# A top-p threshold search with two sums instead of three in the first of two attention steps

## The chip, the cores and the metric

The program runs on one core of one Trainium2 chip. The metric is the device time of one execution in microseconds (us), the median of several. The core has five engines that run side by side and meet at semaphores: TensorE (PE in the profile), VectorE (DVE), ScalarE (ACT), GpSimd (POOL) and SyncE (SP, which here only starts transfers).

## The reference

Four graph layers over 2048 nodes with 128 features follow each other. The change lies in the second, which runs two attention steps:

```python
q = X @ W1.T @ W2.T; k = X @ W3.T
probs = softmax(q @ k.T)                      # 2048 x 2048
idx = argsort(-probs); sp = take_along_axis(probs, idx)
cs = cumsum(sp)
keep_sorted = cs - sp < 0.9                   # top-p: the largest entries until 0.9 is reached
A = probs * mask;  A = A / A.sum(-1)
for n in range(2):   A = top_p(Xa);  Xf = R @ Xf;  Xa = A @ Xa;  Z += Xf @ U1[n].T + Xa @ U2[n].T
```

So in each step every one of the 2048 rows needs the value at which the sum of its larger entries first reaches 0.9 of the row.

## The kernel before

A step is cut into four **groups** of 512 rows, and a group into four **tiles** of 128 rows by 2048 columns (index `k`); `gi` counts the groups, 0 to 3 in the first step and 4 to 7 in the second. The exponentials of a group lie in the buffer EA or EB by turns, so one group's search can run while the previous group is still being multiplied.

For each tile PE makes the logits (line 713, instructions at line 710), DVE takes the row maxima (`row_max`, 1636), and ACT takes the exponential and its row sum (`exponential`, 1187). A first guess of the threshold comes from the mean logit and the row sum (`guess_gap`, 1661; ACT's `guess`, 1204; `guess_first`, 1672).

Then comes the **search**. A sum is the mass of a tile's entries at or above the trial threshold; on DVE it is one pass over 128x2048 (`mass_above`, 1808), on ACT it is two passes, Relu and Sign (`sums_below`, 1216). After the first sum a model of the slope gives a step (`first_step`); after the second and the third a secant gives it (`next_step`, 1877). The flag m == 1, which only the third has, makes the secant lean: the surplus is multiplied by 1.2 or 0.8, whichever is larger, and 7 times the threshold is added (`AHEAD`), so that the threshold comes to lie a few entries above the root. `REACH` and `REACH_HI` limit a step; the limits are constants of one instruction.

In the first group of a step (`BOTH`, gi 0 and 4) `first_sums` (1925) and `third_sum` (1900) run one after the other: three tiles on DVE, the fourth on ACT. In the other groups the first two sums are taken ahead, while the group before is finished: three tiles on ACT and the last on DVE; the third sum then takes all four tiles on DVE.

After the search (`group`, 2049) `under` writes, tile by tile, the entries below the threshold to `cands[k]`; before it writes there, DVE waits until PE has turned the previous group's `cands[k]` (`e_turned`). Eight-wide maxima over eight sets of 256 columns, and four rounds of them, give the 32 largest of these entries; a running sum finds the crossing among them (`crossing_checked`, 1969). `doubtful` (2035) raises a flag where the crossing is not safely inside: threshold at or below the root, no crossing among the first 31, or a set of 256 that may hold more than eight of the wanted entries. One flagged row of the group sends DVE through `surely` (2015), a bracketed search with as many rounds as it needs, each of four sums, followed by four passes of `under`, four of maxima, four of `masked` and four of ties. `masked` (1982) writes the kept entries and their sum, and `kept_ok` releases PE.

The **order of the work** is written out by hand on each engine. While DVE searches group gi, PE multiplies group gi - 1 (`attend`, 756): per tile 16 transposes (line 527; `turns(0)` to `turns(3)`) and 16 products (788), with ACT copying each set of four transposes (1060). Between them PE makes the logits of group gi + 1, one tile per tile (each needs the exponential of the tile before it), and DVE's row maxima of that group are spread over the search: the one of tile 1 (`next_max(1)`) sits inside `third_sum`, that of tile 2 ahead of the first `under`, that of tile 3 after the second `under`. In group 0 there is no earlier group to multiply. There PE runs **units** (line 728; `unit_sums`, 580, instructions at 593) of another product, whose operand SP reloads in two halves per unit, and it makes the logits of group 1 between two units. ACT's order in group 0 is: exponential of a tile of group 1, then the copies of a unit.

Of the kernel before, what the change touches and what calls it, by code (L numbers as in the profile page):

```python
# [7 lines left out]
ALU = mybir.AluOpType  # L8
# [11 lines left out]
G = BK // P  # L20
NB = NT // G
# [7 lines left out]
REACH = 1.2  # L29
REACH_HI = 1.95  # L30
SOFT = (40.0, 20.0)
AHEAD = 7.0
ROUNDING = 2e-5
# [61 lines left out]
def gnn_kernel(nc, x, adj, W0, b0, W1, W2, W3, U1, U2, ln_g, ln_b, L2W, L3W, b3, out):  # L95
# [18 lines left out]
    with ExitStack() as ctx:  # L114
# [202 lines left out]
        def sums_by(gi, m=0):  # L317

            step, g = gi // NB, gi % NB
            each = 2 * (3 + 2 * (G - 1) * (NB - 1))  # L320
            return each * step + (2 * m if g == 0 else 6 + 2 * (G - 1) * (2 * (g - 1) + m))

        def thresholds_by(gi, m=0):

            step, g = gi // NB, gi % NB
            return (3 + 2 * (NB - 1)) * step + (m if g == 0 else 3 + 2 * (g - 1) + m)

# [725 lines left out]
        def _(act):  # L1053
# [284 lines left out]
            for step in range(STEPS):  # L1338
# [8 lines left out]
                for g in range(NB):  # L1347
# [20 lines left out]
                    for k in range(G):  # L1368
                        if g > 0:
                            attend(step, g - 1, k, (lambda: guess(step, g + 1)) if more and k == G - 1 else None, normed,  # L1370
                                   inside=(lambda: exponential(step, g + 1, 1)) if more and k == 0 else None)
                        if g == 0 and k == 1:
                            sums_below(step, 0, 2, (3,))
                        if g == 0 and k > 0:
                            exponential(step, 1, k)
                        if g > 0 and more and 0 < k < G - 1:
                            exponential(step, g + 1, k + 1)
                        if g == 0:
                            if k == G - 1:
                                guess(step, 1)  # L1380
                            unit_next()
# [106 lines left out]
        def _(dve):  # L1488
# [370 lines left out]

            def remember(q, m):  # L1860

# [3 lines left out]
                v.put(dve.tensor_copy(f_old, q.fval))  # L1865
                if m == 1:
                    v.put(ts(ahead, q.th, AHEAD, ALU.mult))

# [7 lines left out]

            def next_step(q, m):


                v.put(tt(den, q.fval, f_old, ALU.subtract))  # L1880
                bounded(q)
                if m == 1:
                    v.put(ts(pb, q.fval, 1.0 - LEAN, ALU.mult))
                v(stt(den, den, -1.0, ALU.mult, den, ALU.max))
                v(tt(den, den, soft, ALU.add))
                if m == 1:
                    v.put(stt(q.fval, q.fval, 1.0 + LEAN, ALU.mult, pb, ALU.max))
                v(dve.reciprocal(den, den))
                if m == 1:
                    v.put(tt(q.fval, q.fval, ahead, ALU.add))  # L1890
                v(tt(q.inv_slope, num, den, ALU.mult))
                v(tt(q.step_u, q.fval, q.inv_slope, ALU.mult))
                stepped(q, REACH_HI if m == 1 else REACH)

# [5 lines left out]
            def third_sum(E, gi, between):  # L1900
# [3 lines left out]
                mass_above(E, gi, 0)  # L1904
                remember(q, 1)
                if gi not in BOTH:
# [12 lines left out]
                else:  # L1919
                    mass_above(E, gi, 3)  # L1920
                    v.wait()
                    surplus(q)
                next_step(q, 1)

            def first_sums(E, gi, between):
# [10 lines left out]
                mass_above(E, gi, 0)  # L1936
                remember(q, 0)
                mass_above(E, gi, 1)
# [6 lines left out]
                shared_surplus(q, gi, 1)  # L1945
                next_step(q, 0)
                dve.sem_inc(th_ok, 1)

# [100 lines left out]
            def group(E, gi, left):  # L2049
# [9 lines left out]
                if gi in BOTH:  # L2059
# [3 lines left out]

                    first_sums(E, gi, early)
                    third_sum(E, gi, lambda: next_max(1))
                else:
                    third_sum(E, gi, lambda: next_max(1))

# [37 lines left out]
                if left > 0:  # L2106
# [4 lines left out]
                    dve.sem_inc(th_ok, 1)  # L2111
                    remember(nq, 0)
                if left > 1:
# [28 lines left out]
                if left > 0:  # L2142
# [4 lines left out]
                    last_surplus(nq)  # L2147
                    next_step(nq, 0)

# [293 lines left out]
```

How the kernel before makes its waits and increments, by code:

```python
    def wait(self, back=0):  # L67
        self.eng.wait_ge(self.sem, self.base + self.n - back)
# [268 lines left out]
        @block.sync  # L338
        def _(sp):
            for s in range(G):
                sp.dma_start(EA[:, s, :], adj_tiles[:, s, :]).then_inc(nat_in[s], 16)
                if s == 0:
                    sp.dma_start(K[:, :, :], x_rows).then_inc(in_x, 16)
            for t in range(G, NT):
                done, count = row_sum_done(t - G)
                sp.wait_ge(at_t, 4 * (t - G + 1))
                sp.wait_ge(done, count)
                sp.dma_start(EA[:, t % G, :], adj_tiles[:, t, :]).then_inc(nat_in[t % G], 16)
            sp.wait_ge(deg_s, 1)
            sp.dma_start(deg_dram, ST[1][0:NT, 0:P]).then_inc(deg_d1, 16)
            sp.wait_ge(deg_d1, 16)
            sp.wait_ge(at_t, 4 * NT)
            sp.dma_start(EA[:, 3, :], deg_dram.rearrange("t p -> (t p)").unsqueeze(0).to_broadcast([P, N]))\
              .then_inc(deg_d2, 16)
            sp.wait_ge(at_out, 4 * NT + 4)
            with sp.Fori(0, UNITS) as u:
                sp.dma_start(keep_at[:, bass.ds(u, 1), :, :], AT[:, bass.ds(u, 1), :, :]).then_inc(at_saved, 16)
            for b in range(NB):
                sp.wait_ge(x1_ok, b + 1)
                sp.dma_start(keep_x1[:, b * G:(b + 1) * G, :], K[:, b * G:(b + 1) * G, :]).then_inc(x1_dma[b], 16)
            sp.wait_ge(at_saved, 16 * UNITS)
            sp.wait_ge(cs_ok, 1)
            sp.wait_ge(ps_mm, NB)
            for u in range(2 * UNITS):
```

## Time and profile before

| what | value |
|---|---|
| three runs | 1050.21 us median (1046.84 to 1052.52) |
| profiled execution, its own time | 1052.0 us |
| its span, first to last instruction | 1050.2 us |
| mean granted clock of TensorE | 0.877 of full |
| busy: PE, DVE, ACT | 811.1, 778.6, 510.8 us |
| chain that ended last: PE, DVE, ACT, issue | 38%, 37%, 11%, 9% of the span |

Instruction times are counted from the start of the span. Busy shares are means over stages with different limits; the first attention step lies between about 161 us, the first sum of group 0, and 497 us, where the second step begins. PE's instruction ends are modelled. "issue" is idle time for which the profile shows nothing waited for.

### The profile page before, as it was taken

How to read it: one execution, taken by the hardware profiler on the slowest of the kernel's cores; microseconds unless marked ns; L12 is line 12 of the kernel's file. 1: busy time of each engine (PE TensorE's matmuls, PEld its weight loads, DVE VectorE, ACT ScalarE, POOL GpSimd, SP SyncE). 2: the span in 40 equal slices, each digit the busy share in tenths (PEclk: the TensorE clock that was granted, in tenths of full speed). 3: DMA queues.
4: the chain of work that ended last, by engine and by line, in shares of the span. 5: the costliest groups of instructions: out<-in, count | busy, mean ns of one | idle time of the engine just before them, and what ended most of it. 6: DMA issues, size and time to landing. Idle time of an engine off the chain costs nothing.

```text
span 1050.2 us, 12275 instructions
## 1 busy us (share of the span) xinstructions
PE 811.1 (77%) x3886; PEld 556.4 (53%) x3886; DVE 778.6 (74%) x2363; ACT 510.8 (49%) x981; POOL 68.0 (6%) x63
## 2 busy tenths in 40 slices
PE   5889947777887853929678968858668999996795
PEld 5744414545665732728266647647356485553342
DVE  5968778988998998970798899799799512325715
ACT  4877235367468476404552754764865232023112
POOL 0020001000000000000000000020101100003201
PEclk9999977888988985959788779979879999998798
DMA  9949304334004000000044220230351447400001
GB/s 338 351 165 432 137 0 161 120 121 161 1 1 161 1 0 2 1 2 1 1 160 148 97 78 1 96 121 1 105 234 41 159 203 297 183 1 0 1 0 40
DMA packets 20221, 108.25 MB, mean 103 GB/s; under 512 B 1824, under 2 KB 8752, under 8 KB 9776
## 3 DMA queue, kind: packets, MB, share of 16 engines
q1 hardware_dynamic: 18752, 106.77, 27.3%
q10 hardware_dynamic: 1392, 0.61, 0.2%
q8 instruction: 29, 0.48, 0.2%
q14 instruction: 48, 0.39, 0.1%
HBM read 88.23 MB, written 19.14 MB: 102 GB/s over the span
## 4 chain that ended last, share of the span: by engine, by line
PE 38%; DVE 37%; ACT 11%; issue 9%; POOL 2%; DVEq 1%; DMA 1%; POOLq 0%; SPq 0%; ACTq 0%
DVE AT L1500 13%; PE PS L788 8%; PE PS L657 5%; DVE mxv L1639 5%; PE PS L527 4%; PE PS L857 3%; DVE AT L2086 3%; DVE nd L1503 3%; ACT BC L1229 3%; PE PS L1038 3%; PE PS L1014 3%; PE PS L710 3%; ACT AT L1229 2%; PE PS L1044 2%; DVE se L1493 2%
## 5 line engine op out<-in xcount | busy, mean ns | idle before, releaser
L1060 ACT ACTIVATE AT<-PS 128x512 f32<-128x512 f32 (+2 forms) x240 | 119.0, 568 | 118.9 <-PE PS L527 100.7
L527 PE MATMUL PS<-ident,AT 128*128 128x128 f32 x544 | 87.6, 298 | 57.8 <-DVE rS L2141 24.4
L1500 DVE SCALAR_TENSOR_TENSOR AT<-EA,se 128x2048 uint8<-128x2048 f32 (+1 forms) x46 | 107.6, 2345 | 1.5 <-DVE se L1493 0.3
L527 PEld LDWEIGHTS PS<-ident,AT 128*128 128x128 f32 x544 | 70.8, 155 | 66.3 <-DVE rS L2141 26.0
L710 PE MATMUL PS<-K,ST 64*128 64x512 f32 x256 | 91.5, 810 | 17.4 <-ACT EA L1197 10.9
L1500 DVE SCALAR_TENSOR_TENSOR AT<-AT 128x2048 uint8<-128x2048 f32 (+2 forms) x48 | 96.1, 2002 | 2.3 <-PE PS L527 1.3
L2086 DVE MAX8 AT<-AT 128x8 f32<-128x256 f32 x256 | 87.6, 412 | 0.7
L1639 DVE TENSOR_REDUCE mxv<-PS 128x1 f32<-128x2048 f32 x32 | 73.2, 2288 | 15.1 <-PE PS L710 14.7
L788 PE MATMUL PS<-AT 128*128 128x128 f32 x512 | 72.4, 292 | 12.5 <-ACT AT L1060 12.0
L788 PE MATMUL PS<-hr,AT 128*128 128x128 f32 x512 | 72.8, 293 | 8.5 <-ACT AT L1060 7.5
L788 PEld LDWEIGHTS PS<-AT 128*128 128x128 f32 x512 | 65.9, 202 | 21.4 <-ACT AT L1060 17.1
L788 PEld LDWEIGHTS PS<-hr,AT 128*128 128x128 f32 x512 | 66.2, 203 | 17.7 <-ACT AT L1060 11.7
L1060 ACT ACTIVATE ST<-PS 128x512 f32<-128x512 f32 (+3 forms) x43 | 24.0, 562 | 100.0 <-PE PS L1044 23.7
L593 PE MATMUL PS<-AT,hr 128*128 128x256 f32 x256 | 61.4, 395 | 5.1 <-DVE gs L1497 4.2
L593 PE MATMUL PS<-AT 128*128 128x256 f32 x256 | 61.3, 394 | 2.8 <-DVE gs L1497 1.6
L593 PEld LDWEIGHTS PS<-AT,hr 128*128 128x128 f32 x256 | 49.3, 198 | 19.2 <-DVE gs L1497 7.3
L710 PEld LDWEIGHTS PS<-K,ST 64*128 64x128 f32 x256 | 30.7, 240 | 52.3 <-issue 45.1
L593 PEld LDWEIGHTS PS<-AT 128*128 128x128 f32 x256 | 49.0, 197 | 16.7 <-issue 6.0
L657 PE MATMUL PS<-AT,R 128*128 128x512 f32 x128 | 56.6, 594 | 1.4 <-DVE R L1493 1.4
L1014 PE MATMUL PS<-AT,R 128*128 128x512 f32 x128 | 57.3, 592 | 0.0
L857 PE MATMUL PS<-AT,hr 128*128 128x512 f32 x96 | 46.8, 641 | 10.3 <-ACT hr L1335 10.3
L1197 ACT ACTIVATE AT<-PS,negmax 128x2048 f32<-128x2048 f32 x16 | 31.5, 1968 | 45.0 <-DVE negmax L1497 44.8
(293 smaller groups left out, 1458.7 us busy)
## 6 DMA issues: line engine op xcount, KB each, us to landing
AT<-keep_at SPq DMA_DIRECT2D x32, 1024.0 KB, 5.1
EA<-in_adj SPq DMA_DIRECT2D x20, 1024.0 KB, 6.4
keep_at<-AT SPq DMA_DIRECT2D x8, 2048.0 KB, 24.8
AT<-keep_at SPq DMA_DIRECT2D x8, 2048.0 KB, 12.4
AT<-in_adj SPq DMA_DIRECT2D x12, 1024.0 KB, 4.9
EA<-keep_degrees SPq DMA_DIRECT2D x1, 1024.0 KB, 6.5
keep_x<-K SPq DMA_DIRECT2D x4, 256.0 KB, 8.6
out<-EA SPq DMA_DIRECT2D x4, 256.0 KB, 2.3
```

Source lines behind the costliest of these rows:

```text
L527: return pe.transpose(dst, src, ident[0:p, 0:p])
L593: mm = pe.matmul(bank(6)[:, 2 * P:4 * P], left[:, j, :], slab[:, j, :], start=(j == 0), stop=(j == NT - 1))
L657: mm = pe.matmul(halves(4 + b % 2), R[:, j, :], AT[:, 2 * b:2 * b + 2, j, :], start=(j == 0), stop=(j == NT - 1))
L710: return pe.matmul(bank(to + n), ST[1][half_rows, k * P:(k + 1) * P], keys[half_rows, n * BK:(n + 1) * BK], start=True, stop=True)
L788: mm = pe.matmul(bank(6)[:, 0:P], stg[b % 2][:, n * P:(n + 1) * P], left[:, j, :], start=(j == 0), stop=(j == NT - 1))
L857: mm = pe.matmul(bank(n), hr[:, t, :], natural(t)[:, n * BK:(n + 1) * BK], start=(t == 0), stop=(t == NT - 1))
L1014: mm = pe.matmul(halves(4 + i % 2), R[:, j, :], AT[:, 2 * b:2 * b + 2, j, :], start=(j == 0), stop=(j == NT - 1))
L1060: return act.activation(dst, src, ACT.Copy)
L1229: act.activation(act_junk[f], E[:, k, :], func, scale=-1.0, bias=th[:, k:k + 1], accum_out=below[:, f, k:k + 1]).then_inc(sum_ok, 1)
L1500: return dve.scalar_tensor_tensor(out=o, in0=x0, scalar=s, in1=x1, op0=op0, op1=op1, **k)
L1639: v(dve.tensor_reduce(mxv[:, odd:odd + 1], PS[:, b:b + 4, :], AX.XY, ALU.max))
L2086: v.put(dve.max(tops[0][:, k, s * TOP:(s + 1) * TOP], cands[k][:, s * N // SETS:(s + 1) * N // SETS]))
```

## The change

`SUMS = (2, 3)` gives the number of sums of each step. Where it is 2, `third_sum` is not called (the row maximum `next_max(1)` that sat inside it is called by itself), ACT's third pair of passes in group 0 is left out, and the second `next_step` is the one that leans, with `AHEAD` 10 in step 0 and 7 as before in step 1. `REACH_HI` goes from 1.95 to 1.99. The counts of semaphores follow.

```diff
--- before.py
+++ after.py
@@ -27,9 +27,10 @@
 D90 = 0.1755
 BEND = 8.0
 REACH = 1.2
-REACH_HI = 1.95
+REACH_HI = 1.99
 SOFT = (40.0, 20.0)
-AHEAD = 7.0
+SUMS = (2, 3)
+AHEAD = (10.0, 7.0)
 ROUNDING = 2e-5
 LEAN = 0.2
 UNIT = 2 * P
@@ -317,13 +318,14 @@
         def sums_by(gi, m=0):
 
             step, g = gi // NB, gi % NB
-            each = 2 * (3 + 2 * (G - 1) * (NB - 1))
-            return each * step + (2 * m if g == 0 else 6 + 2 * (G - 1) * (2 * (g - 1) + m))
+            before = sum(2 * (SUMS[s] + 2 * (G - 1) * (NB - 1)) for s in range(step))
+            return before + (2 * m if g == 0 else 2 * SUMS[step] + 2 * (G - 1) * (2 * (g - 1) + m))
 
         def thresholds_by(gi, m=0):
 
             step, g = gi // NB, gi % NB
-            return (3 + 2 * (NB - 1)) * step + (m if g == 0 else 3 + 2 * (g - 1) + m)
+            before = sum(SUMS[s] + 2 * (NB - 1) for s in range(step))
+            return before + (m if g == 0 else SUMS[step] + 2 * (g - 1) + m)
 
         block = ctx.enter_context(nc.Block())
         raw = hr
@@ -1369,7 +1371,7 @@
                         if g > 0:
                             attend(step, g - 1, k, (lambda: guess(step, g + 1)) if more and k == G - 1 else None, normed,
                                    inside=(lambda: exponential(step, g + 1, 1)) if more and k == 0 else None)
-                        if g == 0 and k == 1:
+                        if g == 0 and k == 1 and SUMS[step] > 2:
                             sums_below(step, 0, 2, (3,))
                         if g == 0 and k > 0:
                             exponential(step, 1, k)
@@ -1857,14 +1859,14 @@
                 v(tt(q.step_u, q.step_u, pa, ALU.mult))
                 stepped(q, REACH)
 
-            def remember(q, m):
+            def remember(q, m, step):
 
 
                 v.put(ts(soft, q.th, SOFT[m], ALU.mult))
                 v.put(stt(num, q.step_u, -1.0, ALU.mult, q.step_u, ALU.max))
                 v.put(dve.tensor_copy(f_old, q.fval))
-                if m == 1:
-                    v.put(ts(ahead, q.th, AHEAD, ALU.mult))
+                if m == SUMS[step] - 2:
+                    v.put(ts(ahead, q.th, AHEAD[step], ALU.mult))
 
             def weigh(q):
 
@@ -1874,23 +1876,23 @@
 
                 v.put(tt(num, num, pa, ALU.add))
 
-            def next_step(q, m):
+            def next_step(q, last):
 
 
                 v.put(tt(den, q.fval, f_old, ALU.subtract))
                 bounded(q)
-                if m == 1:
+                if last:
                     v.put(ts(pb, q.fval, 1.0 - LEAN, ALU.mult))
                 v(stt(den, den, -1.0, ALU.mult, den, ALU.max))
                 v(tt(den, den, soft, ALU.add))
-                if m == 1:
+                if last:
                     v.put(stt(q.fval, q.fval, 1.0 + LEAN, ALU.mult, pb, ALU.max))
                 v(dve.reciprocal(den, den))
-                if m == 1:
+                if last:
                     v.put(tt(q.fval, q.fval, ahead, ALU.add))
                 v(tt(q.inv_slope, num, den, ALU.mult))
                 v(tt(q.step_u, q.fval, q.inv_slope, ALU.mult))
-                stepped(q, REACH_HI if m == 1 else REACH)
+                stepped(q, REACH_HI if last else REACH)
 
             def shared_surplus(q, gi, m):
 
@@ -1902,7 +1904,7 @@
 
                 q = guess_of[gi % 2]
                 mass_above(E, gi, 0)
-                remember(q, 1)
+                remember(q, 1, gi // NB)
                 if gi not in BOTH:
                     between()
                 mass_above(E, gi, 1)
@@ -1920,7 +1922,7 @@
                     mass_above(E, gi, 3)
                     v.wait()
                     surplus(q)
-                next_step(q, 1)
+                next_step(q, True)
 
             def first_sums(E, gi, between):
 
@@ -1934,7 +1936,7 @@
                 dve.sem_inc(th_ok, 1)
                 between()
                 mass_above(E, gi, 0)
-                remember(q, 0)
+                remember(q, 0, gi // NB)
                 mass_above(E, gi, 1)
                 v.wait(1)
                 weigh(q)
@@ -1943,8 +1945,9 @@
                 weighed()
                 v.wait()
                 shared_surplus(q, gi, 1)
-                next_step(q, 0)
-                dve.sem_inc(th_ok, 1)
+                next_step(q, SUMS[gi // NB] == 2)
+                if SUMS[gi // NB] > 2:
+                    dve.sem_inc(th_ok, 1)
 
             def under(w, E, bound, k, **kw):
 
@@ -2062,9 +2065,10 @@
                         next_max(0)
 
                     first_sums(E, gi, early)
+                if SUMS[gi // NB] > 2:
                     third_sum(E, gi, lambda: next_max(1))
                 else:
-                    third_sum(E, gi, lambda: next_max(1))
+                    next_max(1)
 
                 for k in range(G):
                     if gi > 0:
@@ -2109,7 +2113,7 @@
                     last_surplus(nq)
                     first_step(nq)
                     dve.sem_inc(th_ok, 1)
-                    remember(nq, 0)
+                    remember(nq, 0, (gi + 1) // NB)
                 if left > 1:
                     row_max(gi + 2, 0)
                 load_more()
@@ -2145,7 +2149,7 @@
                     last_tile(nq, gi + 1)
                     surplus_below(nq, gi + 1, 1)
                     last_surplus(nq)
-                    next_step(nq, 0)
+                    next_step(nq, SUMS[gi // NB] == 2)
 
             for step in range(STEPS):
                 dve.wait_ge(k_out, 4 * (step + 1))
```

## Rows read from the trace of the kernel before

**Rows 1.** The page: busy time of each engine, and one group of DMA issues.
```profile
PE 811.1 (77%) x3886; PEld 556.4 (53%) x3886; DVE 778.6 (74%) x2363; ACT 510.8 (49%) x981; POOL 68.0 (6%) x63
...
AT<-keep_at SPq DMA_DIRECT2D x32, 1024.0 KB, 5.1
```

**Rows 2.** DVE, groups by line and shape, 161.4 to 472.1 us; columns as on the page.
```profile
L1500 DVE SCALAR_TENSOR_TENSOR AT<-EA,se 128x2048 uint8<-128x2048 f32 x15 | 35.1, 2346 | 0.4 <-DVE se L1497 0.2 <-DVE se L1493 0.2
...
L1500 DVE SCALAR_TENSOR_TENSOR AT<-AT 128x2048 uint8<-128x2048 f32 x12 | 28.2, 2348 | 0.2
...
L1500 DVE SCALAR_TENSOR_TENSOR AT<-AT,s 128x2048 f32<-128x2048 f32 x8 | 18.3, 2348 | 6.6 <-issue 6.6
...
L1500 DVE SCALAR_TENSOR_TENSOR AT<-EA,s 128x2048 f32<-128x2048 f32 x8 | 18.3, 2348 | 3.6 <-issue 3.6
```

**Rows 3.** Timeline of DVE, group 0: start us, duration us, instruction, [idle before, releaser].
```profile
184.40 2.35 DVE L1500 SCALAR_TENSOR_TENSOR AT<-EA,se 128x2048 uint8<-128x2048 f32 x1 [0.16 <-DVE se L1493]
...
191.65 2.28 DVE L1639 TENSOR_REDUCE mxv<-PS 128x1 f32<-128x2048 f32 x1
...
194.06 0.16 DVE L1500 SCALAR_TENSOR_TENSOR se<-below,se 128x4 f32<-128x4 f32 x1
...
197.44 2.35 DVE L1500 SCALAR_TENSOR_TENSOR AT<-EA,se 128x2048 f32<-128x2048 f32 x1
...
212.48 2.29 DVE L1639 TENSOR_REDUCE mxv<-PS 128x1 f32<-128x2048 f32 x1 [3.33 <-PE PS L710]
```

**Rows 4.** Timeline of PE, group 0.
```profile
184.06 6.64 PE L593 MATMUL PS<-AT,hr 128*128 128x256 f32 x30
...
196.55 0.69 PE L527 MATMUL PS<-ident,AT 128*128 128x128 f32 x2 [5.85 <-ACT AT L1060]
...
198.02 3.58 PE L710 MATMUL PS<-K,ST 64*128 64x512 f32 x8
...
202.51 6.64 PE L593 MATMUL PS<-AT,hr 128*128 128x256 f32 x30
...
210.45 1.99 PE L710 MATMUL PS<-K,ST 64*128 64x512 f32 x8
```

**Rows 5.** Timelines of PE, DVE and ACT, group 1.
```profile
272.86 1.99 PE L710 MATMUL PS<-K,ST 64*128 64x512 f32 x8
...
278.06 2.29 DVE L1639 TENSOR_REDUCE mxv<-PS 128x1 f32<-128x2048 f32 x1
...
280.57 1.97 ACT L1197 ACTIVATE EA<-PS,negmax 128x2048 f32<-128x2048 f32 x1
...
299.56 2.35 DVE L1500 SCALAR_TENSOR_TENSOR AT<-AT 128x2048 f32<-128x2048 f32 x1
...
318.60 0.16 DVE L1500 SCALAR_TENSOR_TENSOR se<-below,se 128x4 f32<-128x4 f32 x1 [1.95 <-ACT BC L1229]
```

**Rows 6.** Timelines of ACT, PE and DVE, group 2.
```profile
346.58 1.97 ACT L1197 ACTIVATE AT<-PS,negmax 128x2048 f32<-128x2048 f32 x1 [1.03 <-DVE negmax L1497]
...
376.28 0.60 PE L527 MATMUL PS<-ident,AT 128*128 128x128 f32 x4
...
377.95 2.35 DVE L1500 SCALAR_TENSOR_TENSOR AT<-EA,se 128x2048 f32<-128x2048 f32 x1
...
397.92 2.00 ACT L1229 ACTIVATE AT<-AT 128x2048 uint8<-128x2048 f32 x1 [4.62 <-DVEq L2111]
```

**Rows 7.** Timelines of DVE and PE, group 3, and DVE in the last group of step 1.
```profile
428.00 2.35 DVE L1500 SCALAR_TENSOR_TENSOR AT<-AT 128x2048 f32<-128x2048 f32 x1
...
437.84 0.60 PE L527 MATMUL PS<-ident,AT 128*128 128x128 f32 x4
...
443.04 2.33 DVE L1500 SCALAR_TENSOR_TENSOR AT<-AT 128x2048 f32<-128x2048 f32 x1
...
462.41 2.35 DVE L1500 SCALAR_TENSOR_TENSOR AT<-AT,s 128x2048 f32<-128x2048 f32 x1 [4.76 <-issue]
...
826.60 2.35 DVE L1500 SCALAR_TENSOR_TENSOR AT<-AT,s 128x2048 f32<-128x2048 f32 x1 [6.79 <-issue]
```

## The prediction

> **What bounds the kernel now.** I read the page first: PE is busy 77% and DVE 74% of the span, so neither is the bound throughout [rows 1]. Then DVE's groups by line over the first attention step: 15 + 12 passes of 2.35 us are the sums of the search, 63.3 us in all [rows 2]. The change takes away 15 of these 27: three in group 0, four in each of groups 1 to 3. In that stretch they had hardly an idle time in front of them (0.4 and 0.2 us), which looks as if each were on the path. So I followed the timelines of DVE, PE and ACT group by group, asking at each joint who else was due when DVE arrived. That decides the forecast: in two of the four groups DVE arrives at its joints little later than PE and ACT do.
>
> **What DVE itself loses.** Group 0: the passes and their small steps from 184.40 to 191.65 (7.25 us) and the secant from 194.06 to 197.44 (3.38 us); the row maximum between them stays [rows 3]. That is 10.6 us. The secant that is left takes over the leaning: three more small instructions, one of them waited for, and a fourth for `AHEAD`. The 3.38 us are some 17 such steps, 0.2 us each [rows 3]; the added ones mostly lie under others, so I take 0.3 us per group. Group 0: 10.3 us. Groups 1 to 3: four passes at 2.35, 9.4 us, a secant of 3.2 us beside them, less 0.3: 12.3 us each. DVE sheds 47.2 us. ACT sheds two passes in group 0; it has nothing waiting behind them before the next row maximum, so they count nothing, bounds 0 and 0.5 us. The changed limits and factors are constants of the same instructions and cost nothing.
>
> **Group 0: 7.5 us of 10.3.** With the third sum gone, the row maximum at 191.65 starts at 184.7, and the exponential behind it is done near 189.2. PE's next unit ends at 184.06 + 6.64 = 190.70 and then sat idle 5.85 us, because ACT's order puts that exponential before the unit's copy [rows 4]. This idle time goes. From the end of a unit to the end of the logits behind it, an unhindered case took 212.44 - 209.15 = 3.3 us from the unit at 202.51 to the logits at 210.45 [rows 4]. So these logits end at 194.0 in place of 201.6, 7.6 us earlier, and from there PE runs unit and logits back to back as before. DVE would be ready at 191 and waits for them; its next wait of that kind, at 212.48, moves to 204.9 [rows 3]. I take 7.5 us. What is late next is PE. The two slow rates in these rows bound it: eight logit matmuls took 3.58 us after the idle time and 1.99 us without it [rows 4]. Were they still slow, the gain would be 5.9; were PE no hindrance at all, 10.3. I take the fast row, as PE's idle gap shrinks to about 0.5 us.
>
> The copies and passes of ACT for group 1, the remaining units and the first `kept_ok` follow DVE's `guess_first`, so the whole tail of group 0 moves with it.
>
> **Group 1: 0.1 us of 12.3.** DVE would want the row maximum of tile 2 at 265.8 in place of 278.06. But its logits end at 272.86 + 1.99 = 274.85 [rows 5], in PE's `attend`, whose start (`kept_ok`) is the same. ACT takes that tile's exponential at 280.57, with no idle time before it, behind the copies of `attend`: it gains nothing [rows 5]. The same holds at tile 3. So PE and ACT run as before, DVE waits, and `under` of the last tile, at 299.56, comes about 1 us earlier because it must wait for PE's transposes. Even that is lost: at 318.60 DVE already waits 1.95 us for ACT's sums of group 2 [rows 5], and these start after ACT's copies of the next queries, which close PE's chain. Bounds 0 and 1.0 us; I take 0.1.
>
> **Group 2: 2.1 us of 12.3.** Here ACT waited 1.03 us for DVE's row maximum ahead of the exponential at 346.58 [rows 6]; this wait goes, and `attend` runs 1.0 us earlier from there. PE's last transposes of the group, 376.28 + 0.60 = 376.9, end at 375.9, and `under` of the last tile, now at 377.95, can start there: 2.1 us [rows 6]. No queries stand in ACT's way in this group; ACT waited 4.62 us for DVE's next threshold ahead of its passes at 397.92 [rows 6], so the 2.1 us get through to `kept_ok`. Bounds 1.0 and 3.0.
>
> **Group 3: 4.5 us of 12.3.** No logits or exponentials lie between the tiles here. DVE reaches `under` at 428.00 - 12.3 = 415.7, ahead of PE, and then follows PE's transposes tile by tile. The last of these ends at 437.84 + 0.60 = 438.4; `under` of the last tile starts there in place of 443.04 [rows 7]: 4.5 us, and nothing else waits between there and `masked` at 462.41. Bounds 4.0 and 5.0.
>
> **A jump.** Ahead of that `masked` DVE idles 4.76 us with the cause "issue": it loads four flags and jumps over `surely`. The same code in the last group of step 1 idles 6.79 us [rows 7], while ahead of `masked` in groups 0 to 2, where the jump comes after it, the gap is 1.8 us (3.6 over groups 0 and 2) [rows 2]. Why the same code takes 4.76 and 6.79 these rows don't say; the change removes about a hundred DVE instructions ahead of it. I leave both as they are and keep 1.8 and 6.8 us as the ends for the one in step 0: 3.0 us more gain, 2.0 less.
> The Trainium skill, "Runtime: NRT & Kernel Launch", section "Instruction fetch mechanics", says that a taken branch to a target outside the fetched window stalls until its page is brought in. By that rule removed instructions shift where the pages fall, and the sum would come out between 12.2 and 17.2 us; by the rows left alone it is 14.2.
>
> **Sum.** 7.5 + 0.1 + 2.1 + 4.5 = 14.2 us. The second step starts that much earlier and its code, loads and order are the same, so nothing takes it back. The profiled execution took 1052.0 us: it becomes 1037.8. It stood 1.8 above the median of the runs shown, so the median becomes 1050.2 - 14.2 = 1036.0 us, 1.35% less. Within 0.5%, 5.3 us, a measurement of this kernel can't tell a change from none.
>
> **Rivals.**
> DVE is the bound all through the step, and all 47.2 us count: 1003. For it: 0.4 and 0.2 us of idle time before 27 passes [rows 2]. Against it: the logits at 274.85 and the transposes at 376.9 and 438.4, each of which ends after DVE would want it [rows 5 to 7]. Chance 0.04.
> The Trainium skill, "Perfetto Trace Analysis", section "Identifying the Most-Contended Engine", advises to find the engine with the highest occupancy and optimize that first; followed without its own second step, dependency chains, it gives this rival. By DVE's occupancy in this step it would be 47.2 us, and the rows of three groups speak against it.
>
> The loads hinder the units. Closer together in group 0, units need their operand halves sooner; a half takes 5.1 us to land [rows 1]. The second half of the unit after 190.70 is freed at 190.7 and wanted at about 197.8, the middle of that unit, so some 2 us are to spare. If loads take twice as long there, about 3 us per unit are lost for two units, and group 0 yields 1.5: 1042; if group 2's joint fails too, 1044. Price 6 to 8 us, deciding from a landing above 7 us. Chance 0.09, half of it inside 0.5% of before with the scatter of runs.
>
> The second threshold isn't good enough, and a group takes the long way. In the kernel before none did: the step has 8 + 8 `masked` passes, which is four groups of four tiles and no second set [rows 2]. But that is with three sums. Nothing in the trace shows how far from the root the second sum leaves a row. It decides from a single row: of 2048, one whose threshold falls below the root, or more than 31 entries above it, or with nine wanted entries in one set of 256. For it: one sum fewer, and the lean up to 10 entries also uses up room in the window. Against: a model step and then a secant step should come close on a sum that changes smoothly with the threshold, and 10 of 31 leave room on both sides; that is an argument and no row. Price of one group, estimated from rows: 4 us of small steps to set up; each round four passes at 2.35, some 24 small steps at 0.2 and a load of flags of 1.8, together 16 us; at the end sixteen passes (four kinds, four tiles), 37.6 us. With three rounds that is 90 us, and 1050.2 - 14.2 + 90 = 1126; with a single round 1094. Slower in every form. Chance 0.15.
>
> **How the numbers follow.** The forecast, 1036.0, has 0.72. Its own bounds are the sums of the ends: 5.9 + 0 + 1.0 + 4.0 - 2.0 = 8.9 and 10.3 + 1.0 + 3.0 + 5.0 + 3.0 = 22.3 us, not all at once; with the scatter of the runs, some 2 us, I take 1028 to 1044. That holds the forecast almost whole and most of the load rival, and leaves out the long way and the 47 us. Faster by over 0.5%: 0.72 + 0.04 + 0.04 = 0.80. Within 0.5%: 0.05. Slower: 0.15.
>
> **What the profile would show.** Right: 12 passes of the search on DVE in step 0 in place of 27, still 16 of `masked`; in group 0 PE's idle time of 5.85 us gone and a wait of DVE for logits ahead of the third row maximum, about 3 us; in group 1 a new wait of DVE for logits of some 6 us and the group as long as before, from one `kept_ok` to the next; in group 3 waits of DVE for PE's transposes ahead of each `under`; step 2 starting near 483. Wrong: more than 16 passes of `masked` or any pass of a round in step 0 (the long way); group 1 shortened by much more than a microsecond (DVE was the path after all); waits of PE for slab loads in group 0 (the loads).

## The result, and the profile after

The changed kernel takes 1036.18 us (median of four runs, 1035.75 to 1036.62), beside 1049.38 us (1046.84 to 1052.52) for the kernel before: 13.2 us less, a ratio of 0.9865 with a 95% interval of 0.9834 to 0.9897. The prediction said 1036.0 in a range of 1028 to 1044. The total was met; two of the four terms it is summed from were not, and the experiments and their profiles show which and why. Medians and ratios in this document leave out three executions of the study, of 1600, 1655 and 2569 us, that stood far above all others of the same kernel.

From the page of the changed kernel: the span, the busy time of the engines, and the chain of work that ended last (shares by engine).

```profile
span 1034.6 us, 12154 instructions
...
PE 803.4 (78%) x3886; PEld 550.7 (53%) x3886; DVE 733.7 (71%) x2246; ACT 506.4 (49%) x977; POOL 68.0 (7%) x63
...
PE 47%; DVE 27%; ACT 12%; issue 9%; POOL 1%; DMA 1%; DVEq 1%; POOLq 0%; SPq 0%; ACTq 0%
```

DVE lost 778.6 - 733.7 = 44.9 us of work beside [rows 1] (47.2 were forecast), and the span got 15.6 us shorter. In the chain DVE falls from 37% to 27% and PE rises from 38% to 47%: what was on DVE's account is now largely PE's.

DVE's groups by line and shape over the changed kernel's first step, 165.7 to 458.1 us, the lines that answer to [rows 2]:

```profile
L1502 DVE SCALAR_TENSOR_TENSOR AT<-EA,se 128x2048 uint8<-128x2048 f32 x8 | 18.6, 2349 | 0.3 <-DVE se L1499 0.2
L1502 DVE SCALAR_TENSOR_TENSOR AT<-EA,s 128x2048 f32<-128x2048 f32 x8 | 18.3, 2349 | 3.5 <-issue 3.5
L1502 DVE SCALAR_TENSOR_TENSOR AT<-AT,s 128x2048 f32<-128x2048 f32 x8 | 18.3, 2348 | 6.8 <-issue 6.8
...
L1502 DVE SCALAR_TENSOR_TENSOR AT<-AT 128x2048 uint8<-128x2048 f32 x4 | 9.4, 2352 | 0.1
```

8 + 4 passes of the search stand where 15 + 12 stood, and `masked` is still 8 + 8: no group took the long way.

**Stages.** A group is measured from one group's end to the next, the end being DVE's reciprocal (`rS<-Sk`) behind the four `masked` passes; group 0 begins with its first sum. The head is what lies ahead of that sum, the tail what lies between group 3 and the second step. These are starts read from DVE's timeline of each kernel, in us; the kernels below the second row are told in the next section, and stars mark groups with three sums.

```text
kernel      head     group 0    group 1    group 2    group 3   tail   second step and rest
before     161.41    *95.53*    *78.55*    *73.94*    *62.40*   25.01   553.36
after      165.72     88.74      74.26      70.53      58.81    24.18   552.36
r_before   164.89    *95.41*    *80.76*    *73.95*    *62.42*   23.90   551.97
r_after    163.59     88.85      75.84      69.05      58.79    24.19   552.49
u0         164.56    *96.05*     74.26      70.57      58.50    24.26   552.50
u12        163.99     88.67     *78.38*    *73.98*     58.26    24.10   552.42
u3         161.64     88.70      77.18      70.53     *62.41*   24.08   550.16
pad        163.81     88.79      74.26      70.91      58.47    24.16   552.40
e_in       161.45     87.96      71.93      67.38      58.09    23.86   548.53
e_in2      165.35     89.89      73.81      66.51      59.18    24.34   549.02
b_in       164.81    *95.93*    *78.38*    *73.94*    *62.52*   23.66   548.56
```

From before to after the four groups lost 6.8 + 4.3 + 3.4 + 3.6 = 18.1 us, the tail 0.8 and the rest 1.0, and the head, whose code is the same, gave 4.3 back: 15.6 us of span.

**Where each group stands now.** DVE's waits of the changed kernel, from its timeline: in group 0 the row maxima behind the units' logits, in group 1 the row maxima of tiles 1 and 2, in group 3 `under` of the four tiles and `masked`.

```profile
199.12 2.29 DVE L1641 TENSOR_REDUCE mxv<-PS 128x1 f32<-128x2048 f32 x1 [4.07 <-PE PS L712]
...
209.95 2.29 DVE L1641 TENSOR_REDUCE mxv<-PS 128x1 f32<-128x2048 f32 x1 [3.33 <-PE PS L712]
...
260.82 2.29 DVE L1641 TENSOR_REDUCE mxv<-PS 128x1 f32<-128x2048 f32 x1 [0.16 <-PE PS L712]
270.10 2.29 DVE L1641 TENSOR_REDUCE mxv<-PS 128x1 f32<-128x2048 f32 x1 [6.81 <-PE PS L712]
...
409.39 2.35 DVE L1502 SCALAR_TENSOR_TENSOR AT<-AT 128x2048 f32<-128x2048 f32 x1 [3.95 <-PE PS L529]
415.88 2.35 DVE L1502 SCALAR_TENSOR_TENSOR AT<-AT 128x2048 f32<-128x2048 f32 x1 [1.38 <-PE PS L529]
422.44 2.35 DVE L1502 SCALAR_TENSOR_TENSOR AT<-AT 128x2048 f32<-128x2048 f32 x1 [1.46 <-PE PS L529]
429.01 2.35 DVE L1502 SCALAR_TENSOR_TENSOR AT<-AT 128x2048 f32<-128x2048 f32 x1 [1.45 <-PE PS L529]
448.64 2.35 DVE L1502 SCALAR_TENSOR_TENSOR AT<-AT,s 128x2048 f32<-128x2048 f32 x1 [5.00 <-issue]
```

Most of what DVE was freed of in groups 1 to 3 has become waiting for PE: 6.81 us ahead of tile 2's row maximum in group 1, 8.2 us in all ahead of `under` in group 3. In group 0 PE's wait of 5.85 us [rows 4] is down to 0.47, and its logits run at the short duration:

```profile
189.16 6.64 PE L595 MATMUL PS<-AT,hr 128*128 128x256 f32 x30
196.28 0.44 PE L529 MATMUL PS<-ident,AT 128*128 128x128 f32 x2 [0.47 <-ACT AT L1062]
...
197.09 1.99 PE L712 MATMUL PS<-K,ST 64*128 64x512 f32 x8
```

### The profile page after: what moved, and what is told of

Read it like the earlier page. It is cut to its first block, busy times and chain, and to the rows that moved or that the text cites. A ratio compares the mean times of both kernels' runs of the same rounds, so it can differ in the third digit from the quotient of the medians.

```text
span 1034.6 us, 12154 instructions
## 1 busy us (share of the span) xinstructions
PE 803.4 (78%) x3886; PEld 550.7 (53%) x3886; DVE 733.7 (71%) x2246; ACT 506.4 (49%) x977; POOL 68.0 (7%) x63
## 4 chain that ended last, share of the span: by engine, by line
PE 47%; DVE 27%; ACT 12%; issue 9%; POOL 1%; DMA 1%; DVEq 1%; POOLq 0%; SPq 0%; ACTq 0%
PE PS L790 11%; DVE AT L1502 7%; PE PS L529 6%; PE PS L659 6%; PE PS L712 4%; DVE mxv L1641 4%; PE PS L859 4%; DVE nd L1505 3%; PE PS L1040 3%; PE PS L595 3%; PE PS L1016 3%; ACT BC L1231 3%; ACT AT L1231 3%; PE PS L1046 2%; DVE AT L2090 2%
## 5 line engine op out<-in xcount | busy, mean ns | idle before, releaser
L1502 DVE SCALAR_TENSOR_TENSOR AT<-EA,se 128x2048 uint8<-128x2048 f32 (+1 forms) x39 | 91.1, 2345 | 2.2 <-PE PS L529 1.0
L1502 DVE SCALAR_TENSOR_TENSOR AT<-AT 128x2048 uint8<-128x2048 f32 (+2 forms) x40 | 77.4, 1934 | 10.5 <-PE PS L529 9.8
L790 PE MATMUL PS<-AT 128*128 128x128 f32 x512 | 72.5, 292 | 12.8 <-ACT AT L1062 12.3
L790 PEld LDWEIGHTS PS<-AT 128*128 128x128 f32 x512 | 66.1, 203 | 21.9 <-ACT AT L1062 17.3
L790 PE MATMUL PS<-hr,AT 128*128 128x128 f32 x512 | 70.6, 287 | 9.0 <-ACT AT L1062 8.2
L595 PE MATMUL PS<-AT 128*128 128x256 f32 x256 | 59.2, 385 | 4.1 <-DVE gs L1499 2.8
L859 PE MATMUL PS<-AT,hr 128*128 128x512 f32 x96 | 46.8, 642 | 10.3 <-ACT hr L1337 10.3
## 6 DMA issues: line engine op xcount, KB each, us to landing
AT<-keep_at SPq DMA_DIRECT2D x8, 2048.0 KB, 12.3
```

Source lines behind the costliest of these rows:

```text
L595: mm = pe.matmul(bank(6)[:, 2 * P:4 * P], left[:, j, :], slab[:, j, :], start=(j == 0), stop=(j == NT - 1))
L790: mm = pe.matmul(bank(6)[:, 0:P], stg[b % 2][:, n * P:(n + 1) * P], left[:, j, :], start=(j == 0), stop=(j == NT - 1))
L859: mm = pe.matmul(bank(n), hr[:, t, :], natural(t)[:, n * BK:(n + 1) * BK], start=(t == 0), stop=(t == NT - 1))
L1502: return dve.scalar_tensor_tensor(out=o, in0=x0, scalar=s, in1=x1, op0=op0, op1=op1, **k)
```

## The experiments

### The total once more, and each part undone

The question was how much of the gain lies in which group. `r_after` is the changed kernel again. In the other three `SUMS` is read by group instead of by step (two sums: AHEAD 10; three: 7), and one part at a time gets its third sum back:

```diff
-SUMS = (2, 3)
+SUMS = (3, 2, 2, 2, 3, 3, 3, 3)   # u0
+SUMS = (2, 3, 3, 2, 3, 3, 3, 3)   # u12
+SUMS = (2, 2, 2, 3, 3, 3, 3, 3)   # u3
```

`r_after`, expected: 

> The changed kernel again, unaltered. Both theories expect 1036 us, within 2 us. What it adds is a second profile of the same code. If the 4.3 us that the head (start to the first sum, 161.4 us before and 165.7 us in the first profile of the changed kernel) lost, and the 4.2 us that group 1 gained beyond what I reckoned, come from where TensorE's granted clock rose and fell in that one execution, this profile shows other values for both, 1 us or more away. If they are effects of the change, it shows the same values within 0.5 us.

Measured: 1034.54 us beside 1049.49, ratio 0.986 (0.9827 to 0.9894), 15.0 us less. The gain is confirmed. The second profile has other values for head and group 1, 163.59 us (2.1 less) and 75.84 us (1.6 more): part of both belongs to the single execution.

`u0`, expected: 

> The changed kernel with three sums again in group 0 alone. Chain theory (PE's units and logits take over from DVE): 7.5 us longer than the changed kernel, 1043.7. DVE theory (every sum counts in full): 10.3 us longer. Share theory (the 13.2 us gained fall on the groups as the removed DVE time does, 10.3 of 47.2): 2.9 us longer.

Measured: 1041.5 us, ratio 0.9908 (0.9874 to 0.9941): 7.0 us over `r_after`. Group 0 went from 88.8 to 96.05. The share theory's 2.9 us falls here. The single executions lie between 1035.5 and 1045.48 us, so the median alone does not separate 7.5 from 10.3; the stages below do.

`u12`, expected: 

> The changed kernel with three sums again in groups 1 and 2 alone: eight passes and two secants come back, 24.6 us of DVE time. Chain theory (PE's products with ACT's exponentials and copies bound these groups): 2.2 us longer than the changed kernel, 1038.4. If what group 1 gained in the profile beyond the reckoning belongs to the change: 6 to 8 us longer. DVE theory: 24.6 us longer. Share theory: 6.9 us longer.

Measured: 1041.82 us, ratio 0.9939 (0.9911 to 0.9968): 7.3 us over `r_after`, where the prediction gave groups 1 and 2 together 2.2. Here the prediction fell. The DVE theory, in which every sum counts in full, would have made it 24.6, which fell further. The median fits both the 6 to 8 us of a larger gain in group 1 and the share theory's 6.9; the latter fell with `u0`.

`u3`, expected: 

> The changed kernel with three sums again in group 3 alone. Chain theory (DVE follows PE's transposes tile by tile): 4.5 us longer than the changed kernel, 1040.7; the profile of the changed kernel would make it 3.6 to 3.8. DVE theory: 12.3 us longer. Share theory: 3.4 us longer.

Measured: 1037.52 us, ratio 0.9889 (0.9855 to 0.9924): 3.0 us over `r_after`; group 3 went to 62.41, as in the kernel before. That is nearer to the 3.6 to 3.8 read from the changed kernel's profile than to the 4.5 forecast.

The three parts add to 7.0 + 7.3 + 3.0 = 17.3 us, close to the 15.0 of all of them given the scatter of the runs, so they are nearly independent. The stages say the same with less scatter. Means over the profiles of the table with two sums (without `e_in` and `e_in2`, with `r195` below for groups 0 to 2) and with three: group 0 88.77 and 95.73, group 1 75.28 and 79.02, group 2 70.11 and 73.95, group 3 58.57 and 62.44. The gains are 7.0, 3.7, 3.8 and 3.9 us, 18.4 together.

### Was the head's loss the change's?

`r_before` is the kernel before, once more, with no edit.

Expected: 

> The kernel before, unaltered, for a second profile of it. Its head in the first profile took 161.4 us, and in five kernels with two sums (code of the head unchanged) 161.6 to 165.7. If the head's length is chance (where TensorE's granted clock rises), this profile lies anywhere in that band and group 1 within 2 us of 78.5. If the change lengthens the head, it shows 161.4 again.

Measured: one run of 1055.07 us, whose head took 164.89 us where the first profile of the same kernel took 161.41. Its group 1 took 80.76 us, 0.26 outside the band expected for it. Three heads, of `before`, `u3` and `e_in`, took 161.4 to 161.6 us; TensorE's mean granted clock in them is 0.93. All others of the study took 163.6 to 165.7 with 0.88 to 0.91. So the 4.3 us that the head gave back are chance, and go with the granted clock, not with the change. Windows from the start to the first sum of the kernel before, then of the changed kernel (columns: length, busy time and count of PE, PEld, DVE, ACT and POOL, granted clock, DMA share, GB/s):

```profile
0.00:161.41 161.41, 125.26 (x528) 75.79 (x528) 120.66 (x258) 92.00 (x150) 18.58 (x20) 0.93 0.62 238
```

```profile
0.00:165.72 165.72, 128.47 (x528) 76.39 (x528) 120.63 (x257) 91.82 (x150) 18.57 (x20) 0.89 0.60 232
```

### Is DVE's freed time in groups 1 and 2 really free?

If DVE only waits there now, work put back at that place costs nothing. `pad` adds two passes whose result nobody uses, 4.7 us in each of the two groups:

```diff
                 else:
                     next_max(1)
+                    if gi in (1, 2):
+                        mass_above(E, gi, 0)
+                        mass_above(E, gi, 1)
```

Expected: 

> The changed kernel with two extra sum passes on DVE in group 1 and two in group 2, whose results nobody uses, right behind the row maximum of tile 1: 4 x 2.35 = 9.4 us of DVE time put back, where the profile shows DVE waiting 6.8 us for PE's logits. Chain theory: no change, 0 to 0.5 us longer. DVE theory: 9.4 us longer. If what these groups gained hangs on DVE's work behind the row maximum of tile 1: 3 us or more longer.

Measured: 1033.07 us beside 1052.32, ratio 0.9819 (0.9764 to 0.9875). Groups 1 and 2 took 74.26 and 70.91 us, against 74.26 and 70.53 without the passes: 9.4 us of DVE's work cost nothing measurable. DVE's timeline in group 1 of `pad`:

```profile
258.95 2.29 DVE L1641 TENSOR_REDUCE mxv<-PS 128x1 f32<-128x2048 f32 x1 [0.15 <-PE PS L712]
261.35 2.34 DVE L1502 SCALAR_TENSOR_TENSOR AT<-AT 128x2048 uint8<-128x2048 f32 x1
263.61 2.35 DVE L1502 SCALAR_TENSOR_TENSOR AT<-AT 128x2048 uint8<-128x2048 f32 x1
268.24 2.29 DVE L1641 TENSOR_REDUCE mxv<-PS 128x1 f32<-128x2048 f32 x1 [2.27 <-PE PS L712]
```

The wait ahead of tile 2's row maximum shrinks from 6.81 to 2.27 us, and the row maximum starts 9.3 us after the one before it in both kernels. So of the 12.3 us that the change took out of each of these groups, at least 4.7 are free now, and what counted is not the sum. `pad` put nothing back ahead of tile 1's row maximum; that the pass there counted is read from the timelines (the section on the prediction), and no run puts that pass back by itself.

### Moving the next bound: ACT's order

In the changed kernel tile 2's row maximum in group 1 ends at 270.10 + 2.29 = 272.39, but ACT takes that tile's exponential only at 275.66, behind copies of `attend`. `e_in` changes ACT's order alone: the exponentials of tiles 1 to 3 each go behind the fourth copy of the tile being multiplied.

```diff
-                    if b == 2 and inside:
+                    if b == 3 and inside:
...
-                                   inside=(lambda: exponential(step, g + 1, 1)) if more and k == 0 else None)
+                                   inside=(lambda: exponential(step, g + 1, k + 1)) if more and k < G - 1 else None)
...
-                        if g > 0 and more and 0 < k < G - 1:
-                            exponential(step, g + 1, k + 1)
```

Expected: 

> The changed kernel with another order on ACT alone: the three exponentials of the next group that ACT takes while PE multiplies (tiles 1, 2, 3) each stand behind the fourth copy of a tile's transposes, in place of behind the third copy (tile 1) or behind the whole tile (tiles 2 and 3). No engine's work changes. Chain theory: PE waits 1.4, 1.5 and 2.1 us per group for ACT at these three places in groups 1 and 2 of the changed kernel; of these 5.0 us some 4 go, in two groups of step 0 and, as far as PE binds there, in two of step 1: 8 to 16 us shorter. DVE theory (DVE is still the bound of the groups): no change within 1 us.

Measured: 1025.5 us beside 1052.32, ratio 0.9743 (0.97 to 0.9785). This beats both kernels. ACT's exponentials of group 1, first of the changed kernel, then of `e_in`:

```profile
263.33 1.97 ACT L1199 ACTIVATE EA<-PS,negmax 128x2048 f32<-128x2048 f32 x1 [0.37 <-DVE negmax L1499]
...
275.66 1.96 ACT L1199 ACTIVATE EA<-PS,negmax 128x2048 f32<-128x2048 f32 x1
...
285.51 1.96 ACT L1199 ACTIVATE EA<-PS,negmax 128x2048 f32<-128x2048 f32 x1
```

```profile
259.11 1.96 ACT L1199 ACTIVATE EA<-PS,negmax 128x2048 f32<-128x2048 f32 x1
...
267.77 1.97 ACT L1199 ACTIVATE EA<-PS,negmax 128x2048 f32<-128x2048 f32 x1
...
276.44 1.97 ACT L1199 ACTIVATE EA<-PS,negmax 128x2048 f32<-128x2048 f32 x1
```

From tile 1's to tile 3's exponential 22.2 us became 17.3.

Does this move need the shorter search? `b_in` is the same edit on the kernel before.

Expected: 

> The kernel before (three sums everywhere) with ScalarE's exponentials of tiles 1 to 3 of the next group each moved behind the fourth copy of the tile before, as in e_in, and nothing else. In e_in the move shortened groups 1 and 2 of the changed kernel by some 3 us each and the second step by 4. Theory A, the move's gain needs the shorter search (the third sum's pass on VectorE still holds the first row max of groups 1 and 2, so that earlier exponentials wait behind it): groups 1 and 2 stay within 1.5 us of the kernel before (79.2 and 73.95), only the second step shortens by about 4, and the time is 4 to 6 us under the kernel before, a ratio of 0.994 to 0.996. Theory B, the two gains are separate: groups 1 and 2 shorten by 3 each too and the time is 9 to 12 us under the kernel before, a ratio of 0.988 to 0.991, so that e_in is the sum of two independent changes.

Measured: 1049.92 us beside 1050.56, ratio 0.9989 (0.9968 to 1.0011). Groups 1 and 2 stayed at 78.38 and 73.94 us, as the first theory has it; the gain of 4 to 6 us that it gave to the total doesn't show, and the interval leaves at most 3.4. In its one profile the second step and the rest took 548.56 us, 3.4 and 4.8 less than in the two profiles of the kernel before. ACT's exponentials of tiles 1 to 3 of group 1 in `b_in`:

```profile
271.83 1.97 ACT L1197 ACTIVATE EA<-PS,negmax 128x2048 f32<-128x2048 f32 x1 [1.30 <-DVE negmax L1495]
...
284.21 1.97 ACT L1197 ACTIVATE EA<-PS,negmax 128x2048 f32<-128x2048 f32 x1 [3.61 <-DVE negmax L1495]
...
294.52 1.96 ACT L1197 ACTIVATE EA<-PS,negmax 128x2048 f32<-128x2048 f32 x1
```

With three sums ACT, moved forward, waits 1.30 and 3.61 us for DVE's row maxima, which stand behind the passes of the third sum. So in the first step the two changes are not independent: the shorter search opens the room that the move uses.

`e_in2` is `e_in` once more, to tell the move's gain from chance.

Expected: 

> The kernel of e_in once more. Its profile had group 1 at 71.93, group 2 at 67.38 and groups 1 and 2 of the second step at 78.67 and 77.74. The last two sums also came near that without the move (78.60 and 77.17 in a7h, 78.66 and 79.94 in u3, 81.23 and 78.75 in the changed kernel), so the second step's gain may be chance. Theory A, the move shortens all four groups: all of these come again within 0.5 us, and the time is 1023 to 1028. Theory B, only groups 1 and 2 of the first step are the move's, and the second step's length is the granted clock's chance: 71.9 and 67.4 again, the second step's two groups anywhere from 156 to 160 together, time 1026 to 1031. Theory C, all was chance: groups 1 and 2 return to 74.3 to 75.9 and 69.1 to 70.9, time 1033 to 1036.

Measured: 1025.02 us beside 1049.21, ratio 0.9754 (0.971 to 0.9798). Groups 1 and 2 took 73.81 and 66.51 us, together 140.3 (139.3 in `e_in`; 144.8 to 145.2 in `after`, `r_after`, `u0` and `pad`, 147.7 in `u3`), so the move shortens these groups by some 5 us. Groups 1 and 2 of the second step took 156.4 us together in all three profiles with the move (`e_in`, `e_in2`, `b_in`) and 158.5 to 160.0 in the eight others of the table; but in the three kernels of the next section, which don't have the move, they took 155.8. So it is not shown that the second step's part of the gain is the move's. The time fits the first theory; group 1, 1.9 us longer than in `e_in`, fits neither of the first two.

### What keeps the rows off the long way

The prediction gave 0.15 to a group taking the long way, and could not say how near that was. The change also aims higher (`AHEAD` 10, `REACH_HI` 1.99). Three kernels, with two sums in the first step, put these constants back: both, the limit alone, the aim alone. Each kernel ran once; its values stand on one line here.

```diff
-REACH_HI = 1.99
-AHEAD = (10.0, 7.0)
+REACH_HI = 1.95; AHEAD = (7.0, 7.0)    # a7
+REACH_HI = 1.95; AHEAD = (10.0, 7.0)   # r195
+REACH_HI = 1.99; AHEAD = (7.0, 7.0)    # a7h
```

`a7`, expected: 

> Two sums in step 0, but aiming as before: AHEAD 7 and REACH_HI 1.95. If the larger lean is what keeps the rows out of the long way, at least one group takes it: 16 or 12 of the passes of masked show in addition, with rounds, and the time is 60 us or more longer than the changed kernel. If the second sum leaves enough room without it: no change, within 2 us.

Measured: 1368.15 us. Groups 1 and 3 took 232.47 and 240.80 us, 157 and 182 more than with the changed constants.

`r195`, expected: 

> The changed kernel with REACH_HI back at 1.95 and AHEAD at 10 in the first step. In a7 both constants were put back and groups 1 and 3 went the long way (232.5 and 240.8 us). Theory A, AHEAD is what keeps the rows on the short way: all four groups as in the changed kernel, span 1030 to 1036. Theory B, the bound on the step (REACH_HI) is what does it: one or two groups take the long way again at 158 to 182 us each, span 1190 to 1370.

Measured: 1209.17 us. Group 1 took 75.85, group 3 240.78 us.

`a7h`, expected: 

> The changed kernel with AHEAD back at 7 in the first step and REACH_HI at 1.99. Theory A, AHEAD is what keeps the rows on the short way: one or two groups take the long way at 158 to 182 us each, span 1190 to 1370. Theory B, the bound on the step does it: span 1030 to 1036. If this run and r195 both stay on the short way, either constant alone is enough; if both leave it, both are needed.

Measured: 1374.29 us. Groups 1 and 3 took 235.55 and 240.90 us.

So neither theory holds by itself: group 1 is kept on the short way by the larger `AHEAD`, and group 3 only by both constants together. DVE's groups in group 3 of `r195`, 397.5 to 638.3 us, show where the time goes:

```profile
L1502 DVE SCALAR_TENSOR_TENSOR AT<-AT,new 128x2048 uint8<-128x2048 f32 x28 | 64.2, 2349 | 17.8 <-issue 17.8
L1502 DVE SCALAR_TENSOR_TENSOR AT<-AT,s 128x2048 f32<-128x2048 f32 x16 | 36.9, 2349 | 11.5 <-issue 11.4
...
L1502 DVE SCALAR_TENSOR_TENSOR AT<-AT,br 128x2048 f32<-128x2048 f32 x4 | 9.1, 2346 | 2.7 <-issue 2.7
L2030 DVE MAX8 AT<-AT 128x8 f32<-128x2048 f32 x4 | 8.9, 2280 | 0.2 <-DVEq L1731 0.2
```

28 passes with a new threshold are seven rounds of four; the prediction had reckoned with one to three. By its own prices seven would make 4 + 7 x 16 + 37.6 = 154 us, an estimate, beside the 182 by which the group grew.

## Why the prediction was right, and where it was not

**The reading that decided held.** DVE shed some 45 us and the groups shortened by 18.4, although almost no idle time stood ahead of its passes [rows 2]: as the prediction had it, PE and ACT were little ahead of DVE at the joints of groups 1 and 2, and became the path there. By the Trainium skill, "Perfetto Trace Analysis", section "Identifying the Most-Contended Engine", as the prediction weighed it, all 47.2 us would have counted; the measured 13 to 15 us speak against that use of it, and `pad` does too, in which 9.4 us of such work cost nothing.

**Group 0: right, 7.5 forecast, 7.0 in the stages and in the medians.** PE's 5.85 us of idle time went, PE runs unit and logits back to back, and DVE waits 4.07 us ahead of the third row maximum, where some 3 were forecast.

**Group 1: the step that failed, 0.1 forecast, 3.7 measured.** The working asked about the row maxima of tiles 2 and 3 and concluded "So PE and ACT run as before". It left out the row maximum of tile 1. That one stands behind the first pass of the third sum, and in the profile of before it looked harmless. DVE and then PE of the kernel before, around the end of group 0 (256.94):

```profile
257.40 2.35 DVE L1500 SCALAR_TENSOR_TENSOR AT<-AT 128x2048 uint8<-128x2048 f32 x1
263.02 2.35 DVE L1500 SCALAR_TENSOR_TENSOR AT<-AT 128x2048 uint8<-128x2048 f32 x1
265.67 2.29 DVE L1639 TENSOR_REDUCE mxv<-PS 128x1 f32<-128x2048 f32 x1
```

```profile
235.59 8.24 PE L593 MATMUL PS<-AT,hr 128*128 128x256 f32 x30
...
261.85 3.79 PE L710 MATMUL PS<-K,ST 64*128 64x512 f32 x8 [3.58 <-ACT EA L1197]
```

The logits end at 261.85 + 3.79 = 265.64 and DVE's pass at 263.02 + 2.35 = 265.37: both are in time for 265.67, and taking the pass away seemed to change nothing. But the logits were late in this execution. The unit shown took 8.24 us (granted clock 0.80) where others take 6.64, and ACT, which copies the units' results, came to the exponential ahead of these logits at 259.64, 2.70 after the end of group 0; in `r_before`, `u12` and `b_in` it came 0.26 after. Without that delay the same place looks like this with three sums (`u12`, group 0 ends at 252.66), DVE and then PE:

```profile
253.12 2.35 DVE L1502 SCALAR_TENSOR_TENSOR AT<-AT 128x2048 uint8<-128x2048 f32 x1
258.68 2.35 DVE L1502 SCALAR_TENSOR_TENSOR AT<-AT 128x2048 uint8<-128x2048 f32 x1
261.24 2.28 DVE L1641 TENSOR_REDUCE mxv<-PS 128x1 f32<-128x2048 f32 x1
```

```profile
255.12 3.78 PE L712 MATMUL PS<-K,ST 64*128 64x512 f32 x8 [0.26 <-ACT EA L1199]
```

The logits end at 258.90, and the row maximum still starts at 261.24, 8.58 us after the end of group 0: the pass holds it. With two sums it starts at 260.82 - 254.46 = 6.36: 2.2 us earlier, and ACT's next exponential, PE's next logits and the tiles of `attend` follow it. So DVE's pass was on the path of group 1 in the three other profiles with three sums there, and in the one that the prediction read PE happened to be just as late. Some 1.4 us more come later in the group, where PE is faster after the change: at 266.35 in `u12`, behind a wait of 3.59 us for ACT, eight products take 2.08 us (granted clock 0.50), and at 293.26 in the kernel before 1.95 (0.56), while at 288.34 in the changed kernel they take 1.16 (1.00). Whether that is a consequence of the shorter waits or chance was not separated.

That is PE's side. On DVE's side no wait is marked in group 1 of `u12` and `b_in` up to `under` of tile 3, and their starts agree (8.58, 20.96 and 42.47 us behind the end of group 0) although ACT's order differs: with three sums DVE is the path of this stretch, and PE follows close. PE's last transposes for that `under` and DVE's pass, first `u12`, then the changed kernel:

```profile
293.17 0.60 PE L529 MATMUL PS<-ident,AT 128*128 128x128 f32 x4
295.13 2.35 DVE L1502 SCALAR_TENSOR_TENSOR AT<-AT 128x2048 f32<-128x2048 f32 x1
```

```profile
291.33 0.60 PE L529 MATMUL PS<-ident,AT 128*128 128x128 f32 x4
291.97 2.35 DVE L1502 SCALAR_TENSOR_TENSOR AT<-AT 128x2048 f32<-128x2048 f32 x1 [0.23 <-PE PS L529]
```

From the end of group 0 the transposes are done at 41.11 and DVE comes at 42.47; with two sums it is 37.47 and 37.51. DVE was 1.4 us behind PE, about what the prediction took, but PE's transposes, which it held for fixed, came 3.6 us earlier. Of the 5.0 us together some 0.8 are lost at the next wait for ACT's sums (1.93 us in `u12`, 2.70 after the change), where the prediction had all of it lost.

**Group 2: right in the mechanism, mis-sized, 2.1 forecast, 3.8 measured.** The same row maximum of tile 1 holds ACT's exponential at 346.58 [rows 6], 11.09 us after the end of group 1. The prediction took only ACT's idle time ahead of it, 1.03 us; in `r_before` and `u12` ACT waits 2.38 and 2.51 us at the same place, so the profile read was again one in which another engine was late. ACT, then DVE at `under` of the last tile, in the changed kernel:

```profile
337.46 1.97 ACT L1199 ACTIVATE AT<-PS,negmax 128x2048 f32<-128x2048 f32 x1 [1.49 <-DVE negmax L1499]
...
367.75 2.35 DVE L1502 SCALAR_TENSOR_TENSOR AT<-EA,se 128x2048 f32<-128x2048 f32 x1 [1.02 <-PE PS L529]
```

The exponential came at 337.46 - 328.72 = 8.74, 2.35 us earlier, because what ACT does ahead of it came earlier too; `under`, which now waits for PE, starts 3.4 us earlier.

**Group 3: right, 4.5 forecast, 3.9 in the stages, 3.0 in the medians.** DVE follows PE tile by tile, as forecast (waits of 3.95, 1.38, 1.46 and 1.45). PE took 2.08 us for the first eight products where it took 1.56 before, and the jump 5.00 in place of 4.76.

**The jump.** 5.00 us where 4.76 was taken. In the eleven profiles of the table it lies between 4.76 and 5.04, and the one in the last group of the second step between 5.99 and 7.65; in `r195` the latter is 4.82. For the first step the bounds of 1.8 and 6.8 were too wide. The shift of pages that the Trainium skill, "Runtime: NRT & Kernel Launch", section "Instruction fetch mechanics", would lead one to look for is at most 0.3 us here; that is no test of its cause.

**The total was met better than its parts.** The terms came to 18.4 us in the stages in place of 14.2, and the medians lost 13.2 and 15.0 us. Part of the difference is that the profiled executions of the kernel before took 1052.0 and 1055.07 us, 2.6 and 2.8 above the medians beside them, those of the changed kernel 1036.4 and 1034.54, within 0.3 of theirs. The rest, a microsecond or two, lies within the intervals and stays open. So the agreement of 1036.0 with 1036.18 to 0.2 us is luck; a sum with group 1 right would have said about 1032 and would have been held by the same range.

**The rivals.** The loads did not hinder the units: group 0 gained what it should. The long way was not taken, and its chance of 0.15 was rested on an argument and no row. The runs show that it was near: with either constant left as it was, a group takes it, at 157 to 182 us per group where 90 were estimated for three rounds. The prediction had counted `AHEAD` as a use of room in the window, against the change; together with the larger `REACH_HI` it is what makes two sums enough here.

## What to carry to other kernels

When one engine's work is cut, look at each instruction of another kind that stands behind the removed work on the same engine, however small, and ask who waits for it; two arrivals that agree within a third of a microsecond in one profile are a reason to look for a second profile, because either may be the later one in the next execution. Time that a cut leaves as a wait is an offer: here it let ACT's order be moved forward, for some 8 to 11 us more, of which some 5 lie in groups 1 and 2 of the first step, where the move alone had given nothing; that the rest is the move's is not shown. Where a cheaper search goes with a changed aim, measure the aim by itself, since it can decide whether an expensive fallback is taken.

## What was not expected of the hardware

The same code ahead of the first sum took 161.4 to 165.7 us from execution to execution, a third of what the medians gained, in step with TensorE's mean granted clock of 0.93 or 0.88 to 0.91 there. The two levels (1.2 and 2.4 GHz) can be read off single rows: eight logit matmuls take 1.99 or 3.78 us, and in the changed kernel, `u12` and `e_in` the first ones behind the end of group 0 take 3.78, at a granted clock of 0.50 in the changed kernel and in `u12` (PE had idled 4.67 and 4.61 us shortly before). Group 1 alone, with the same two sums, took 74.3 to 77.2 us. One profile can't show a term smaller than that.
